# A recurrent layer on one core: the second half's z in three bf16 parts, summed on VectorE

## The chip, the cores and the metric

The kernel runs on one core of a Trainium2 chip. The metric is the device time of one execution in microseconds. Three runs of the kernel before give a median of 1635.45 us.

## The reference

A gated recurrence over 512 steps, for 8 sequences and 512 features, all float32. The input is added to the outputs at the end.

```python
xT = jnp.swapaxes(x, 0, 1)                       # x: (8, 512, 512)
def step(h, x_t):
    fused = jax.nn.sigmoid(jnp.concatenate([x_t, h], axis=-1) @ w_W + w_b)
    hidden_state, output_state = jnp.split(fused, 2, axis=-1)
    memory_state = x_t @ wx_W + wx_b + hidden_state * (h @ wh_W + wh_b)
    h_new = output_state * h + (1.0 - output_state) * jnp.tanh(memory_state)
    return (h_new, h_new)
_, hs = jax.lax.scan(step, h0, xT)
x = x + jnp.swapaxes(hs, 0, 1)
```

Below, r is the gate `hidden_state`, z the gate `output_state`, and m the product `h @ wh_W + wh_b` that r multiplies. Each step needs the h of the step before, so nothing of the recurrence can be done ahead; only the products with x can.

## The kernel before, in words

The 512 features lie as 4 chunks (k = 0 to 3) of 128 partitions. The outputs of a step are made in two halves, o = 0 and o = 1, of two chunks each (W = 64 columns per gate and half). TensorE works with h as the stationary operand, 8 columns (one for each sequence), and the weights as the moving one. Each product is cut into four tiles (j) of 32 array columns side by side, so that each writes 8 rows at 32 j in PSUM, and four matmuls with 64 columns each give 256 features.

Each group has its own PSUM bank: m of the first half (bank 0), r of the first half (1), z of the first half (2), r and m of the second half together (3) and z of the second half (4). ScalarE puts the x products and biases of the step into these banks beforehand (`put_first`, `put_rm`, `put_z`), and all matmuls add to them (`start=False`).

Two kinds of product with h stand side by side:

- `products` (L269 to L276): float32 matmuls of h with `wh`, 8x64, for r, m and z of the first half and for z of the second half. In the order of instructions a step has 64 of them; the trace has two records for each.
- `products_of_parts` (L278 to L287): h in three bf16 parts (24 stationary columns: 8 sequences times 3 parts) with `w_parts`, the weights in three bf16 parts, 24x128, for r and m of the second half. The three parts of h give three groups of 8 rows in PSUM, which VectorE adds (`sum_parts`, L446). GpSimd cuts h into its parts (`part`, L541 to L547), ScalarE and VectorE cut the weights ahead of the loop (L417, L420, L524 to L530).

Of every product the first half of the sum over k (chunks 0 and 1) needs only the first half of h, the second (chunks 2 and 3) only the second half. So TensorE has, in one step (L326 to L353):

```python
r(0, s); m(0, s); z(0, 0, s)     # chunks 0, 1; behind h_ready[0]
products_of_parts(0, s)          # behind parts_ready[0]
r(1, s); m(1, s); z(0, 1, s)     # chunks 2, 3; behind h_ready[1]
products_of_parts(1, s)          # behind parts_ready[1]; rm_done
z(1, 0, s); z(1, 1, s)           # the second half's z; z_done[1]
x_products(s, x_grp[:, s, :])    # a quarter of the next x products
```

The order on each engine is written out by hand, and each engine takes its instructions in that order. When r, m and z of the first half are done, VectorE turns them (32x32 transposes) to features on partitions: `turn_r`, `turn_m`, `turn_z(0)`, L474 to L478. ScalarE takes the sigmoid of r (`reset_first`), VectorE multiplies and adds m (`mix_m(0)`, a scan), ScalarE has the sigmoid of z (`update(0)`) and the tanh (`new(0)`). Then, after rm_done, VectorE has (L482 to L494): `turn_rm`, `sum_parts(0)` (r), `mix_h(0)` (a scan, which gives the first half of h and sets h_ready[0]), `sum_parts(1)` (m), `turn_z(1)`, `mix_m(1)`, `mix_h(1)` (h_ready[1]). ScalarE has in the same time (L396 to L405): `put_first`, `reset_second`, `put_rm`, `update(1)` (sigmoid of z, L375), `new(1)` (tanh, L381), `put_z`. `mix_h` waits for both tanh_ready and z_ready. Once in four steps VectorE adds the bias to the x products behind `mix_h(1)` (`add_bias`, L466). The x products go to a buffer in HBM and back on the DMA queue of SyncE; neither is near the change.

Of the kernel before, what the change touches and what calls it, by code (L numbers as in the profile page):

```python
# [6 lines left out]
ALU = mybir.AluOpType  # L7
# [3 lines left out]
P = 128  # L11
Q = 32


def build(nc, x, h0, w_h, w_x, b_x, b_h, x_rows, out):
# [24 lines left out]
    R_AT = W  # L40
    Z_AT = [2 * W, 3 * W]
    RM_AT = 4 * W
    WHOLE = RM_AT

    M_BANK, R_BANK, RM_BANK = 0, 1, 3
    Z_BANK = [2, 4]
# [18 lines left out]
    with ctx:  # L65
        def sb(name, shape, dt=F32):
            return ctx.enter_context(nc.sbuf_tensor(name, shape, dt))
# [4 lines left out]
        def halves(name):  # L72
            return [sem(f"{name}{o}") for o in range(HALVES)]
# [15 lines left out]
        turned_m = sb("turned_m", [P, ROWS // PAIR, HB, PAIR])  # L89
        turned_rm = sb("turned_rm", [P, 2 * HC, Q])  # L90
        turned_z = sb("turned_z", [P, HALVES, HC, Q])

        summed = sb("summed", [P, 2, HB, PAIR])

# [73 lines left out]
        rm_ahead = sem("rm_ahead")  # L168
        z_ahead = sem("z_ahead")
        r_ready = halves("r_ready")  # L170
        z_ready = halves("z_ready")
        m_pre_ready = halves("m_pre_ready")
        tanh_ready = halves("tanh_ready")
# [86 lines left out]
        @block.tensor  # L260
        def _(pe):
            def x_products(k, stands, bank=X_BANK):

                for j in range(TILES):
                    mm = pe.matmul(ps[Q * j:Q * (j + 1), bank, 0:COLS], stands, wx[:, k, j, :],  # L265
                                   start=(k == 0), stop=(k == KC - 1), tile_position=(0, Q * j))
                return mm

            def products(bank, at, half, s):  # L269


                for k in range(half * HC, (half + 1) * HC):
                    for j in range(TILES):
                        mm = pe.matmul(ps[Q * j:Q * j + B, bank, 0:W], h_of(s - 1, k), wh[:, k, j, at:at + W],  # L274
                                       start=False, stop=(k == KC - 1), skip_group_check=True, tile_position=(0, Q * j))
                return mm  # L276

            def products_of_parts(half, s):  # L278

                for k in range(half * HC, (half + 1) * HC):  # L280
                    for part in range(PARTS):
                        for j in range(TILES):
                            mm = pe.matmul(ps[Q * j:Q * j + PARTS * B, RM_BANK, 0:2 * W], parts_of(s - 1, k),  # L283
                                           w_parts[:, k, part, j], start=False,
                                           stop=(k == KC - 1 and part == PARTS - 1), skip_group_check=True,
                                           tile_position=(0, Q * j))
                return mm  # L287

            def m(half, s):
                return products(M_BANK, M_AT[0], half, s)  # L290

            def r(half, s):
                return products(R_BANK, R_AT, half, s)

            def z(o, half, s):
                return products(Z_BANK[o], Z_AT[o], half, s)

            zeros = h.rearrange("p r o w -> p (r o w)")  # L300
            pe.wait_ge(start_h, 1)
            for n in range(WARM):
                for j in range(TILES):
                    pe.matmul(ps[Q * j:Q * (j + 1), X_BANK, 0:COLS], zeros[:, 0:Q], zeros[:, 0:COLS],
                              start=True, stop=True, tile_position=(0, Q * j))
            for bank in range(X_BANK):
                for j in range(TILES):
                    mm = pe.matmul(ps[Q * j:Q * (j + 1), bank, 0:2 * W], zeros[:, 0:Q], zeros[:, 0:2 * W],
                                   start=True, stop=True, tile_position=(0, Q * j))
            mm.then_inc(bits_set, 1)  # L310
            pe.wait_ge(x0_loaded, 16)
            for k in range(KC):
                pe.wait_ge(wx_loaded[k], 16)
                for g in range(2):
                    last = x_products(k, x_sb[:, k, GT * g:GT * (g + 1)], X_BANK + g)
                    if k == KC - 1:
                        last.then_inc(x_product, 1)
            pe.wait_ge(wh_loaded, KC * 16)
            pe.wait_ge(first_cut, KC)
            pe.wait_ge(second_cut, KC)  # L320
            pe.wait_ge(third_cut, KC)

            with nc.Fori(0, GROUPS, engines=(mybir.EngineType.PE,), hint_back_edge=True) as i:
                t0 = pe.snap(i * RING)
                for s in range(RING):
                    nxt = held(pe, t0 + (s + 1))  # L326
                    pe.wait_ge(h_ready[0], nxt)
                    pe.wait_ge(first_ahead, nxt)
                    r(0, s)
                    if s == 0:  # L330
                        loaded = held(pe, i * 16 + 16)
                    m(0, s)
                    if s == 0:
                        taken = held(pe, i + 2)
                    z(0, 0, s)
                    pe.wait_ge(parts_ready[0], nxt)
                    pe.wait_ge(rm_ahead, nxt)
                    products_of_parts(0, s)
                    pe.wait_ge(h_ready[1], nxt)
                    r(1, s).then_inc(r_done, 1)  # L340
                    m(1, s).then_inc(m_done, 1)
                    z(0, 1, s).then_inc(z_done[0], 1)
                    pe.wait_ge(parts_ready[1], nxt)
                    products_of_parts(1, s).then_inc(rm_done, 1)
                    pe.wait_ge(z_ahead, nxt)
                    z(1, 0, s)
                    z(1, 1, s).then_inc(z_done[1], 1)
                    pe.wait_ge(x_grp_loaded[s], loaded)
                    if s == 0:
                        pe.wait_ge(x_biased, taken)  # L350
                    last = x_products(s, x_grp[:, s, :])
                    last.then_inc(x_used[s] if s < RING - 1 else x_product, 1)

        @block.scalar
        def _(act):
# [7 lines left out]
            def put_z(slot, t):  # L363
                at = Z_AT[1]
                act.activation(ps[:, Z_BANK[1], 0:W], ahead[:, slot, t, at:at + W], ACT.Copy).then_inc(z_ahead, 1)
# [6 lines left out]
                act.activation(m_by[:, 1, :, 1], summed[:, 0, :, 0], ACT.Sigmoid).then_inc(r_ready[1], 1)  # L372

            def update(o):
                act.activation(h_by[:, o, :, 2].rearrange("p (b c) -> p c b", c=HC), turned_z[:, o, :, 0:B], ACT.Sigmoid)\  # L375
                    .then_inc(z_ready[o], 1)

            def new(o, s):
# [5 lines left out]
            def step(i, t0, s):  # L384
                nxt = held(act, t0 + (s + 1))
                slot, t = (s + 1) // RING % SLOTS, (s + 1) % RING
                if t == 0:
                    turn = held(act, (i * (PER_BLOCK // SLOTS) + ((s + 1) // RING // SLOTS + 1)) * LANDED)
                act.wait_ge(r_turned, nxt)
                reset_first()  # L390
                act.wait_ge(z_turned[0], nxt)
                update(0)
                act.wait_ge(m_pre_ready[0], nxt)
                new(0, s)
                if t == 0:
                    act.wait_ge(ahead_loaded[slot], turn)  # L396
                put_first(slot, t)
                act.wait_ge(r_summed, nxt)
                reset_second()
                put_rm(slot, t)  # L400
                act.wait_ge(z_turned[1], nxt)
                update(1)
                act.wait_ge(m_pre_ready[1], nxt)
                new(1, s)
                put_z(slot, t)  # L405

            act.dma_start(bias_x[:, :], b_x).then_inc(bias_x_loaded, 16)
# [24 lines left out]
        def _(dve):  # L432
# [13 lines left out]
            def sum_parts(g):  # L446
                return dve.tensor_reduce(summed[:, g, :, 0].rearrange("p (c b) -> p c b", b=B),  # L447
                                         turned_rm[:, HC * g:HC * (g + 1)].rearrange("p c (w b) -> p c b w", b=B)
                                         [:, :, :, 0:PARTS], AX.X, ALU.add)

            def mix_m(o, add):

                return dve.tensor_tensor_scan(m_pre[:, o].rearrange("p i w -> p (i w)"),  # L453
                                              m_by[:, o].rearrange("p i w -> p (i w)"),
                                              add.rearrange("p i w -> p (i w)"), 0.0, ALU.mult, ALU.add)

            def mix_h(o, s, nxt):

                dve.wait_ge(tanh_ready[o], nxt)
                dve.wait_ge(z_ready[o], nxt)  # L460
                dve.tensor_tensor_scan(h[:, s % RING, o, 0:REGION], h_by[:, o].rearrange("p i w -> p (i w)"),  # L461
                                       h[:, (s - 1) % RING, o, 1:1 + REGION], 0.0, ALU.mult, ALU.add)\
                    .then_inc(h_ready[o], 1)
# [4 lines left out]
            def step(i, t0, s):  # L468
# [22 lines left out]
                dve.wait_ge(x_moved, nxt)  # L491
                dve.wait_ge(m_summed, nxt)
                mix_m(1, summed[:, 1]).then_inc(m_pre_ready[1], 1)
                mix_h(1, s, nxt)  # L494
                if s % RING == RING - 1:

# [143 lines left out]
```

## Time and profile before

| what | value |
|---|---|
| runs | 1635.45 us median of 3 (1634.96 to 1636.28) |
| the profiled execution | 1634.35 us, span 1632.2 us |
| granted TensorE clock, mean | 0.995 |
| TensorE matmul, busy | 1603.5 us, 98% of the span, 94336 records |
| TensorE weight load, busy | 1377.4 us, 84% |
| VectorE, busy | 1162.8 us, 71% |
| ScalarE, busy | 910.0 us, 56% |
| GpSimd, busy | 682.3 us, 42% |
| DMA | 51 GB/s mean |
| chain that ended last | TensorE 97%, DMA 1% |
| of it by line | L274 (float32 products) 56%, L283 (parts) 21%, L265 (x) 20% |

The busy shares are for the whole span, in which some 30 us ahead of the loop are mostly loading. The chain is followed back from the last instruction, at each step to what released it. It says which engine was waited for, not how close the next one was. The time of the profiled execution is 2.1 us above its span; sums are made against 1634.35.

### The profile page before, as it was taken

How to read it: one execution, taken by the hardware profiler on the slowest of the kernel's cores; microseconds unless marked ns; L12 is line 12 of the kernel's file. 1: busy time of each engine (PE TensorE's matmuls, PEld its weight loads, DVE VectorE, ACT ScalarE, POOL GpSimd, SP SyncE). 2: the span in 40 equal slices, each digit the busy share in tenths (PEclk: the TensorE clock that was granted, in tenths of full speed). 3: DMA queues.
4: the chain of work that ended last, by engine and by line, in shares of the span. 5: the costliest groups of instructions: out<-in, count | busy, mean ns of one | idle time of the engine just before them, and what ended most of it. 6: DMA issues, size and time to landing. Idle time of an engine off the chain costs nothing.

```text
span 1632.2 us, 213115 instructions
## 1 busy us (share of the span) xinstructions
PE 1603.5 (98%) x94336; PEld 1377.4 (84%) x94336; DVE 1162.8 (71%) x5782; ACT 910.0 (56%) x4621; POOL 682.3 (42%) x3084
## 2 busy tenths in 40 slices
PE   5899999999999999999999999999999999999998
PEld 3788888888888888888888888888888888888887
DVE  3677777777777777777777777777777777777776
ACT  2455555555555555555555555555555555555555
POOL 1344444444444444444444444444444444444443
PEclk7999999999999999999999999999999999999999
DMA  6111111111111111111111111111111111111111
GB/s 203 31 51 48 52 37 49 47 53 50 47 39 51 49 47 54 37 47 52 51 48 48 40 50 47 52 51 47 39 50 50 47 53 38 48 52 50 49 47 41
DMA packets 194891, 83.29 MB, mean 51 GB/s; under 512 B 123200, under 2 KB 194368, under 8 KB 194880
## 3 DMA queue, kind: packets, MB, share of 16 engines
q1 hardware_dynamic: 193824, 82.47, 18.7%
q10 hardware_dynamic: 1056, 0.67, 0.2%
q8 instruction: 6, 0.10, 0.0%
q14 instruction: 5, 0.04, 0.0%
HBM read 49.30 MB, written 33.75 MB: 51 GB/s over the span
## 4 chain that ended last, share of the span: by engine, by line
PE 97%; DMA 1%; issue 0%; ACT 0%; ACTq 0%; DVE 0%; SPq 0%; POOL 0%; POOLq 0%; DVEq 0%
PE ps L274 56%; PE ps L283 21%; PE ps L265 20%; DMA wx<-in_w_x 1%; DMA x_rows<-xs_biased 0%; ACTq L198 0%; ACT w_parts L417 0%; ACTq L194 0%; ACT w_parts L420 0%; SPq L211 0%; SPq L209 0%; DVE xs_biased L466 0%; DVE h L461 0%; DVE turned_rm L441 0%; POOL y L554 0%
## 5 line engine op out<-in xcount | busy, mean ns | idle before, releaser
L274 PE MATMUL ps<-wh,h 128*8 128x64 f32 x65536 | 1218.0, 219 | 20.0 <-ACT ps L357 14.6
L274 PEld LDWEIGHTS ps<-wh,h 128*8 128x8 f32 x65536 | 1030.9, 92 | 238.8 <-DVE h L461 216.4
L283 PE MATMUL ps<-w_parts,h 128*24 128x128 bf16 x24576 | 544.1, 219 | 0.0
L283 PEld LDWEIGHTS ps<-w_parts,h 128*24 128x24 bf16 x24576 | 442.8, 121 | 0.0
L265 PE MATMUL ps<-wx,x_grp 128*32 128x384 f32 x4096 | 430.7, 486 | 0.0
L368 ACT ACTIVATE m_by<-turned_r 128x16 f32<-128x16 f32 x512 | 112.0, 219 | 561.4 <-DVE turned_r L434 561.4
L544 POOL TENSOR_TENSOR h<-h 128x16 f32<-128x16 f32 x1026 | 224.4, 219 | 365.5 <-DVE h L461 361.9
L461 DVE TENSOR_TENSOR_SCAN h<-h_by,h 128x48 f32<-128x48 f32 x1024 | 260.6, 254 | 160.9 <-ACT h L381 160.9
L576 POOL TENSOR_TENSOR summed<-turned_rm,nothing 128x16 f32<-128x16 f32 x512 | 113.5, 222 | 498.6 <-DVE turned_rm L441 498.6
L434 DVE STREAM_TRANSPOSE turned_r<-ps 128x64 f32<-128x64 f32 x512 | 128.1, 250 | 262.9 <-PE ps L274 258.4
L375 ACT ACTIVATE h_by<-turned_z 128x16 f32<-128x16 f32 x1024 | 238.5, 233 | 117.9 <-DVE turned_z L444 63.2
L546 POOL TENSOR_TENSOR h<-h 128x16 f32<-128x16 f32 x1026 | 225.0, 219 | 80.4
L381 ACT ACTIVATE h<-m_pre 128x32 f32<-128x32 f32 x1024 | 252.7, 247 | 0.0
L444 DVE STREAM_TRANSPOSE turned_z<-ps 128x64 f32<-128x64 f32 x1024 | 247.9, 242 | 2.9 <-PE ps L274 2.9
L447 DVE TENSOR_REDUCE summed<-turned_rm 128x16 f32<-128x48 f32 x1024 | 197.1, 192 | 17.4
L357 ACT ACTIVATE ps<-ahead 128x192 f32<-128x192 f32 x513 | 171.6, 335 | 0.0
L441 DVE STREAM_TRANSPOSE turned_rm<-ps 128x128 f32<-128x128 f32 x512 | 162.1, 317 | 0.3 <-PE ps L283 0.3
L554 POOL TENSOR_TENSOR y<-x_sb,h 128x32 f32 x512 | 137.9, 269 | 0.9
L361 ACT ACTIVATE ps<-ahead 128x128 f32<-128x128 f32 x513 | 135.1, 263 | 0.0
L437 DVE STREAM_TRANSPOSE turned_m<-ps 128x64 f32<-128x64 f32 x512 | 119.5, 233 | 1.5 <-PE ps L274 1.4
L372 ACT ACTIVATE m_by<-summed 128x16 f32<-128x16 f32 x512 | 112.1, 219 | 14.5 <-DVE summed L447 0.4
L453 DVE TENSOR_TENSOR_SCAN m_pre<-m_by,summed 128x32 f32<-128x32 f32 x512 | 115.0, 225 | 0.0
(29 smaller groups left out, 429.4 us busy)
## 6 DMA issues: line engine op xcount, KB each, us to landing
x_rows<-xs_biased SPq DMA_DIRECT2D x128, 192.0 KB, 1.9
ahead<-x_rows SPq DMA_DIRECT2D x512, 32.0 KB
ahead<-x_rows SPq DMA_DIRECT2D x1024, 8.0 KB
x_sb<-in_x SPq DMA_DIRECT2D x34, 256.0 KB, 3.1
x_grp<-in_x SPq DMA_DIRECT2D x516, 16.0 KB, 1.7
out_h<-y SPq DMA_DIRECT2D x32, 256.0 KB, 2.7
wx<-in_w_x SPq DMA_DIRECT2D x4, 768.0 KB, 9.1
wh<-in_w_h SPq DMA_DIRECT2D x4, 512.0 KB, 7.3
```

Source lines behind the costliest of these rows:

```text
L265: mm = pe.matmul(ps[Q * j:Q * (j + 1), bank, 0:COLS], stands, wx[:, k, j, :], start=(k == 0), stop=(k == KC - 1), tile_position=(0, Q * j))
L274: mm = pe.matmul(ps[Q * j:Q * j + B, bank, 0:W], h_of(s - 1, k), wh[:, k, j, at:at + W], start=False, stop=(k == KC - 1), skip_group_check ...
L283: mm = pe.matmul(ps[Q * j:Q * j + PARTS * B, RM_BANK, 0:2 * W], parts_of(s - 1, k), w_parts[:, k, part, j], start=False, stop=(k == KC - 1 ...
L357: act.activation(ps[:, 0:GATES, 0:W], ahead[:, slot, t, 0:GATES * W].rearrange("p (g n) -> p g n", n=W), ACT.Copy).then_inc(first_ahead, 1)
L375: act.activation(h_by[:, o, :, 2].rearrange("p (b c) -> p c b", c=HC), turned_z[:, o, :, 0:B], ACT.Sigmoid)\
L381: act.activation(n_twice, pre.unsqueeze(3).to_broadcast([P, HC, B, 2]), ACT.Tanh)\
L441: return dve.transpose(turned_rm[:, :, :], ps[:, RM_BANK, 0:2 * W].rearrange("p (c q) -> p c q", q=Q))
L444: return dve.transpose(turned_z[:, o], ps[:, Z_BANK[o], 0:W].rearrange("p (c q) -> p c q", q=Q))
L447: return dve.tensor_reduce(summed[:, g, :, 0].rearrange("p (c b) -> p c b", b=B), turned_rm[:, HC * g:HC * (g + 1)].rearrange("p c (w b) - ...
L461: dve.tensor_tensor_scan(h[:, s % RING, o, 0:REGION], h_by[:, o].rearrange("p i w -> p (i w)"), h[:, (s - 1) % RING, o, 1:1 + REGION], 0.0 ...
L544: pool.tensor_tensor(mid(1, s, o), mid(0, s, o), mid_top(0, s, o), ALU.subtract).then_inc(left_once[o], 1)
L546: pool.tensor_tensor(mid(2, s, o), mid(1, s, o), mid_top(1, s, o), ALU.subtract)\
```

## The change

The second half's z goes over from `products` to `products_of_parts`. Its weights are cut into bf16 parts too (`w_rest` and `w_parts` grow from 128 to 192 columns per tile, `wh` shrinks from 256 to 192). z keeps a bank and a group of its own with 64 columns, so a matmul there is 24x64. Its 8-row groups must now be added: `sum_z` on VectorE, between `mix_m(1)` and `mix_h(1)`, into the new tile `pre_z`, with the semaphore z_summed. `update(1)` reads `pre_z`, waits for z_summed, and stands behind `new(1)` on ScalarE. `mix_h(1)` waits for z_ready first and tanh_ready second.

```diff
-    WHOLE = RM_AT
+    WHOLE = Z_AT[1]
...
+        pre_z = sb("pre_z", [P, HC, B])
...
-            def products_of_parts(half, s):
+            def products_of_parts(bank, at, cols, half, s):
 
                 for k in range(half * HC, (half + 1) * HC):
                     for part in range(PARTS):
                         for j in range(TILES):
-                            mm = pe.matmul(ps[Q * j:Q * j + PARTS * B, RM_BANK, 0:2 * W], parts_of(s - 1, k),
-                                           w_parts[:, k, part, j], start=False,
+                            mm = pe.matmul(ps[Q * j:Q * j + PARTS * B, bank, 0:cols], parts_of(s - 1, k),
+                                           w_parts[:, k, part, j, at - WHOLE:at - WHOLE + cols], start=False,
                                            stop=(k == KC - 1 and part == PARTS - 1), skip_group_check=True,
...
-            def z(o, half, s):
-                return products(Z_BANK[o], Z_AT[o], half, s)
+            def z(half, s):
+                return products(Z_BANK[0], Z_AT[0], half, s)
+
+            def second_rm(half, s):
+                return products_of_parts(RM_BANK, RM_AT, 2 * W, half, s)
+
+            def second_z(half, s):
+                return products_of_parts(Z_BANK[1], Z_AT[1], W, half, s)
...
                     pe.wait_ge(parts_ready[1], nxt)
-                    products_of_parts(1, s).then_inc(rm_done, 1)
+                    second_rm(1, s).then_inc(rm_done, 1)
                     pe.wait_ge(z_ahead, nxt)
-                    z(1, 0, s)
-                    z(1, 1, s).then_inc(z_done[1], 1)
+                    second_z(0, s)
+                    second_z(1, s).then_inc(z_done[1], 1)
...
             def update(o):
-                act.activation(h_by[:, o, :, 2].rearrange("p (b c) -> p c b", c=HC), turned_z[:, o, :, 0:B], ACT.Sigmoid)\
+                pre = (turned_z[:, 0, :, 0:B], pre_z[:, :, :])[o]
+                act.activation(h_by[:, o, :, 2].rearrange("p (b c) -> p c b", c=HC), pre, ACT.Sigmoid)\
                     .then_inc(z_ready[o], 1)
...
                 put_rm(slot, t)
-                act.wait_ge(z_turned[1], nxt)
-                update(1)
                 act.wait_ge(m_pre_ready[1], nxt)
                 new(1, s)
+                act.wait_ge(z_summed, nxt)
+                update(1)
                 put_z(slot, t)
...
+            def sum_z():
+                return dve.tensor_reduce(pre_z[:, :, :],
+                                         turned_z[:, 1].rearrange("p c (w b) -> p c b w", b=B)[:, :, :, 0:PARTS],
+                                         AX.X, ALU.add)
+
...
-                dve.wait_ge(tanh_ready[o], nxt)
-                dve.wait_ge(z_ready[o], nxt)
+                for ready in ((tanh_ready[o], z_ready[o]), (z_ready[o], tanh_ready[o]))[o]:
+                    dve.wait_ge(ready, nxt)
...
                 mix_m(1, summed[:, 1]).then_inc(m_pre_ready[1], 1)
+                dve.wait_ge(z_turned[1], nxt)
+                sum_z().then_inc(z_summed, 1)
                 mix_h(1, s, nxt)
```

ScalarE, the second half of a step, before (`summed` is r of the second half, `m_pre` what the tanh is taken of):

```order
L372 ACTIVATE m_by<-summed 128x16 [waits r_summed]
L361 ACTIVATE ps<-ahead 128x128
L375 ACTIVATE h_by<-turned_z 128x2x8 [waits z_turned1]
L381 ACTIVATE h<-m_pre 128x2x8x2 [waits m_pre_ready1]
L365 ACTIVATE ps<-ahead 128x64
```

and with the change:

```order
L380 ACTIVATE m_by<-summed 128x16 [waits r_summed]
L369 ACTIVATE ps<-ahead 128x128
L390 ACTIVATE h<-m_pre 128x2x8x2 [waits m_pre_ready1]
L384 ACTIVATE h_by<-pre_z 128x2x8 [waits z_summed]
L373 ACTIVATE ps<-ahead 128x64
```

The sigmoid of z has moved behind the tanh, and waits for VectorE's sum instead of the transpose.

VectorE, from the second half's sum of m to the end of the step, before (both scans are printed as SCALAR_TENSOR_TENSOR):

```order
L447 TENSOR_REDUCE summed<-turned_rm 128x16
L444 STREAM_TRANSPOSE turned_z<-ps 128x64 [waits z_done1]
L453 SCALAR_TENSOR_TENSOR m_pre<-m_by,summed 128x32 [waits m_summed,x_moved,r_ready1]
L461 SCALAR_TENSOR_TENSOR h<-h_by,h 128x48 [waits z_ready1,tanh_ready1]
L470 REGISTER_ALU
```

and with the change:

```order
L456 TENSOR_REDUCE summed<-turned_rm 128x16
L453 STREAM_TRANSPOSE turned_z<-ps 128x64 [waits z_done1]
L467 SCALAR_TENSOR_TENSOR m_pre<-m_by,summed 128x32 [waits m_summed,x_moved,r_ready1]
L461 TENSOR_REDUCE pre_z<-turned_z 128x16 [waits z_turned1]
L475 SCALAR_TENSOR_TENSOR h<-h_by,h 128x48 [waits tanh_ready1,z_ready1]
L484 REGISTER_ALU
```

One reduction has come in between the two scans; nothing else has changed place.

TensorE, from the second half's r to the x product, before:

```order
L274 MATMUL ps<-wh,h 8x64 [waits h_ready1]
L274 MATMUL ps<-wh,h 8x64 x23
L283 MATMUL ps<-w_parts,h 24x128 [waits parts_ready1]
L283 MATMUL ps<-w_parts,h 24x128 x23
L274 MATMUL ps<-wh,h 8x64 [waits z_ahead]
L274 MATMUL ps<-wh,h 8x64 x15
```

and with the change:

```order
L276 MATMUL ps<-wh,h 8x64 [waits h_ready1]
L276 MATMUL ps<-wh,h 8x64 x23
L285 MATMUL ps<-w_parts,h 24x128 [waits parts_ready1]
L285 MATMUL ps<-w_parts,h 24x128 x23
L285 MATMUL ps<-w_parts,h 24x64 [waits z_ahead]
L285 MATMUL ps<-w_parts,h 24x64 x47
```

The 16 float32 matmuls of the second half's z are 48 bf16 ones in the same place.

## Rows read from the trace of the kernel before

PE is TensorE's matmul, PEld its weight load, DVE VectorE, ACT ScalarE, POOL GpSimd, SP SyncE.

**Rows 1.** Busy us (x records) by engine in a stretch; PE clock, DMA share, GB/s

```profile
100.00:1600.00 1500.00, 1500.00 (x88985) 1294.04 (x88978) 1089.41 (x5443) 854.37 (x4356) 639.69 (x2901) 1.00 0.18 48
```

**Rows 2.** Order in time, PE, one step: start us, us covered, line, xrecords

```profile
801.16 0.64 PE L274 MATMUL ps<-wh,h 128*8 128x64 f32 x32
801.61 0.84 PE L265 MATMUL ps<-wx,x_grp 128*32 128x384 f32 x8
802.25 0.87 PE L274 MATMUL ps<-wh,h 128*8 128x64 f32 x48
802.92 0.53 PE L283 MATMUL ps<-w_parts,h 128*24 128x128 bf16 x24
803.26 0.87 PE L274 MATMUL ps<-wh,h 128*8 128x64 f32 x48
803.93 0.53 PE L283 MATMUL ps<-w_parts,h 128*24 128x128 bf16 x24
804.26 0.25 PE L274 MATMUL ps<-wh,h 128*8 128x64 f32 x4
```

**Rows 3.** Order in time, the first matmuls of the loop

```profile
30.59 1.22 PEld L274 LDWEIGHTS ps<-wh,h 128*8 128x8 f32 x48 [15.29 <-issue]
30.62 1.47 PE L274 MATMUL ps<-wh,h 128*8 128x64 f32 x48 [14.62 <-ACT ps L357]
```

**Rows 4.** Waits: who for whom, us in total, times, longest us

```profile
PEld ps L274 <- DVE h L461: 216.4, 509, 0.4
```

**Rows 5.** Order in time, DVE, ACT and PEld, the step's end

```profile
801.49 0.23 ACT L381 ACTIVATE h<-m_pre 128x32 f32<-128x32 f32 x1
801.61 0.33 ACT L357 ACTIVATE ps<-ahead 128x192 f32<-128x192 f32 x1
...
801.87 0.25 DVE L461 TENSOR_TENSOR_SCAN h<-h_by,h 128x48 f32<-128x48 f32 x1
802.04 0.18 DVE L447 TENSOR_REDUCE summed<-turned_rm 128x16 f32<-128x48 f32 x1
...
802.35 0.23 DVE L453 TENSOR_TENSOR_SCAN m_pre<-m_by,summed 128x32 f32<-128x32 f32 x1
802.41 0.23 ACT L375 ACTIVATE h_by<-turned_z 128x16 f32<-128x16 f32 x1
802.61 0.25 ACT L381 ACTIVATE h<-m_pre 128x32 f32<-128x32 f32 x1
802.75 0.23 ACT L365 ACTIVATE ps<-ahead 128x64 f32<-128x64 f32 x1
802.89 0.26 DVE L461 TENSOR_TENSOR_SCAN h<-h_by,h 128x48 f32<-128x48 f32 x1 [0.32 <-ACT h L381]
803.21 0.73 PEld L274 LDWEIGHTS ps<-wh,h 128*8 128x8 f32 x48
```

**Rows 6.** Order in time, PEld, cut off at 802.20

```profile
802.17 0.11 PEld L274 LDWEIGHTS ps<-wh,h 128*8 128x8 f32 x4 [0.42 <-DVE h L461]
```

**Rows 7.** Order in time, the parts of the second half's h

```profile
803.53 0.22 POOL L546 TENSOR_TENSOR h<-h 128x16 f32<-128x16 f32 x1
...
803.87 0.43 PEld L283 LDWEIGHTS ps<-w_parts,h 128*24 128x24 bf16 x24
```

**Rows 8.** Groups by line: shapes xcount | busy us, mean ns | idle before

```profile
L274 PEld LDWEIGHTS ps<-wh,h 128*8 128x8 f32 x65536 | 1030.9, 92 | 238.8 <-DVE h L461 216.4 <-issue 22.3
L375 ACT ACTIVATE h_by<-turned_z 128x16 f32<-128x16 f32 x1024 | 238.5, 233 | 117.9 <-DVE turned_z L444 63.2
L368 ACT ACTIVATE m_by<-turned_r 128x16 f32<-128x16 f32 x512 | 112.0, 219 | 561.4 <-DVE turned_r L434 561.4
L417 ACT ACTIVATE w_parts<-w_rest 128x512 bf16<-128x512 f32 x4 | 2.2, 617 | 22.0 <-issue 22.0
```

**Rows 9.** Order in time, DVE, the end of a group of four steps

```profile
809.29 0.56 DVE L466 TENSOR_TENSOR xs_biased<-ps,bias_x 128x384 f32<-128x384 f32 x1
810.03 0.25 DVE L434 STREAM_TRANSPOSE turned_r<-ps 128x64 f32<-128x64 f32 x1 [0.18 <-PE ps L274]
```

More of the change, by code:

```diff
@@ L170, in build @@
         r_ready = halves("r_ready")
+        z_summed = sem("z_summed")
         z_ready = halves("z_ready")
@@ L334, in _ @@
                         taken = held(pe, i + 2)
-                    z(0, 0, s)
+                    z(0, s)
                     pe.wait_ge(parts_ready[0], nxt)
                     pe.wait_ge(rm_ahead, nxt)
-                    products_of_parts(0, s)
+                    second_rm(0, s)
                     pe.wait_ge(h_ready[1], nxt)
@@ L341, in _ @@
                     m(1, s).then_inc(m_done, 1)
-                    z(0, 1, s).then_inc(z_done[0], 1)
+                    z(1, s).then_inc(z_done[0], 1)
                     pe.wait_ge(parts_ready[1], nxt)
-                    products_of_parts(1, s).then_inc(rm_done, 1)
+                    second_rm(1, s).then_inc(rm_done, 1)
                     pe.wait_ge(z_ahead, nxt)
-                    z(1, 0, s)
-                    z(1, 1, s).then_inc(z_done[1], 1)
+                    second_z(0, s)
+                    second_z(1, s).then_inc(z_done[1], 1)
                     pe.wait_ge(x_grp_loaded[s], loaded)
```

## The prediction, made before the change was run

> **What bounds the kernel now.** I first read busy time and clock. From 100 to 1600 us TensorE (PE) is busy 1500.00 of 1500.00 us, at a granted clock of 1.00, the 2.4 GHz level [rows 1]; the chain of waits, too, is PE almost throughout (the table above). The reader is to see an engine without a gap in the steady state. But "busy" with modelled ends can hide short waits, so the next view is the order in time [rows 2]. I take start-to-start, never the durations: 48 records are given 0.87 us, but the next kind starts 0.67 after them, since neighbours overlap in the array. A float32 matmul leaves two records. One step runs from the start of the first half's r to the next such start. Its pieces: 48 records of r, m, z from 802.25 to 802.92, 0.67 us; 24 of the parts to 803.26, 0.34; 48 more to 803.93, 0.67; 24 more to 804.26, 0.33; the second half's z, which the change rewrites, 32 records from 801.16 to 801.61, 0.45; the x product, 801.61 to 802.25, 0.64. The sum is **3.10 us**: the period is PE's work alone. 512 x 3.10 = 1587, the first matmul is at 30.62 [rows 3], and the rest of the span is the first steps, at a lower clock.
>
> Is anything just behind PE? PE's weight loads waited for the scan of h 509 times, 216.4 us in all [rows 4]: once in a step, for the first half's h. For the second half's h nothing is recorded. The order in time shows how close both are. The scan of the first half ends at 801.87 + 0.25 = 802.12 [rows 5], the load follows at 802.17 [rows 6] and the matmul at 802.25 [rows 2]. The scan of the second half ends at 802.89 + 0.26 = 803.15, its load follows at 803.21 [rows 5], the matmul at 803.26. A load stands 0.05 to 0.06 before its matmul also where nothing is waited for (parts: load 803.87 [rows 7], matmul 803.93). So the second half's h comes just in time. How little a load needs ahead of its matmul when PE is idle: 30.59 to 30.62, 0.03 us [rows 3]. The slack of the second half is thus 803.26 - 803.21 - 0.03 = **0.02 us**, that of the first half 0.08 - 0.03 = 0.05.
>
> **The change, part by part.**
>
> *PE, second half's z.* 16 float32 matmuls of 64 columns (32 records, 0.45 us) become 48 bf16 ones of 24x64. No row has that shape. Nearest: 24 bf16 pairs of 24x128 take 0.33 to 0.34 us [rows 2], 0.014 each. If the price goes by columns, 48 with half the columns take 0.34; if it goes by pairs, 48 x 0.014 = 0.67. Which? The float32 records of 64 columns take 0.67/48 = 0.014 too. They show only that 0.014 for a pair of load and matmul can be held. The weight loads alone come faster: four in 0.11 us [rows 6], where one takes 0.092 [rows 8], so some 0.006 apart. That is nearer to the low end; I take 0.34 to 0.45, and keep 0.67 for the range. PE's own work becomes 3.10 - 0.45 + 0.34 = 2.99 to 3.10.
>
> The Trainium skill (TensorE: Matmul & The Clock Gate, Back-to-back issue gap) gives columns/2.4 + 2.5 ns for a lone stream, never below about 25 ns, but about 81 ns a matmul at 128 columns for a stream of load and matmul. By that second figure, four tiles side by side, 24 pairs would take 0.49 us; this trace has 0.34, which is the first formula (55.8 ns for four). By the first, the new z would be 12 x 29.2 ns = 0.35 us, an estimate from that page; a pace of loads and matmuls that columns do not lower would be rival (1).
>
> *The wait for the first half's h.* Its scan hangs on rm_done, turn_rm, sum, scan, none of which is changed. PE arriving up to 0.11 sooner can win at most the 0.05 of slack: 3.05.
>
> *ACT and DVE, second half.* This is the term that decides. Before, the sigmoid of z stood ahead of the tanh, 802.41 to 802.64, in time in which ACT waited for the scan of m anyway. That scan ends at 802.35 + 0.23 = 802.58, the tanh starts at 802.61 and ends at 802.86, and the scan of h starts at 802.89 [rows 5]. So the tanh hung on the scan of m, not on the sigmoid, and taking the sigmoid from in front of it wins nothing. Now the sigmoid comes behind the tanh, and the scan of h waits for it. When can it start? (a) For ACT's sake: the next instruction behind the tanh (put_z) starts at 802.75, 0.14 after it. (b) For the sum's sake: DVE gets on 0.17 after the start of the longer scan of h (801.87 to 802.04), so sum_z runs from 802.52 at the latest, takes 0.18 like the second sum of parts, and reaches ACT 0.03 later, at 802.73. So (a) decides, the sum itself is covered with 0.02 to spare, and without this cover its lateness would be added one to one. Sigmoid from 802.75, 0.23 long [rows 8], ends at 802.98; scan of h from 803.01 instead of 802.89: **0.12 us later**. It is bounded from below by a sigmoid of 0.22 (those of r [rows 8]) with a gap of 0.12 (801.49 to 801.61, tanh to put_first): 0.09 later. From above, with a sum that starts when the scan of m has ended (802.58) and so ends at 802.79 with the latency: 0.16 later.
>
> *Who waits for that.* The second half's r, m and z on PE. h ends at 803.27, the load comes at 803.33, the matmul at 803.36 at the earliest: 0.10 after 803.26. From there to rm_done is 72 records as before, and from rm_done to the scans the same path as before: the ring closes, and PE's 0.11 saved lies outside it, between rm_done and h. The period is 3.10 + 0.12 - 0.02 = **3.20 us**. Bounds: 3.10 + 0.09 - 0.02 = 3.17 and, with all the lateness and no slack, 3.10 + 0.16 = 3.26. PE, on its own at 2.99 to 3.10, is below it and waits 0.1 to 0.2 in each step.
>
> *Neighbours.* The parts on POOL hang on the same h: the second subtraction, from 803.53, is done at 803.75, where the load of parts is at 803.87 [rows 7]; POOL moves by 0.12, the load by 0.10, covered. add_bias on DVE, once in four steps, ends at 809.29 + 0.56 = 809.85, ahead of the turn of r at 810.03 [rows 9]; both move alike, covered. put_z is later by 0.12 and used over a microsecond later: nothing. turn_z sits behind sum_parts(1) on DVE, long after z's end: nothing.
>
> *Ahead of the loop.* w_rest grows from 512 to 768 columns. The eight casts on ACT lead to put_first and to the first matmul. ACT's slope, from a cast of 512 columns [rows 8] and put_z's 64 [rows 5], is (617 - 230)/448 = 0.86 ns a column, so 256 more cost 0.22 us each, 8 x 0.22 = **1.8 us**. DVE's subtractions between them grow at a like rate and keep ahead. Bounds 0 and 4.
>
> *Sum.* 512 steps x 0.10 = 51.2, and 1.8: 1634.35 + 53.0 = 1687.4 for an execution like the profiled one (span 1632.2, 2.1 around it); the median shown, 1635.45, is 1.1 above it, so **1688.5**. Case bounds: 512 x 0.07 + 0 gives 1671; 512 x 0.16 + 4 gives 1721, of which I keep up to 1716, the last 0.01 needing every bound at once.
>
> **The rivals.**
>
> (1) *A pair has a price of its own.* If 48 pairs of 64 columns take 0.67, PE needs 3.32 a step: 512 x 0.22 + 2 = 115, 1750 us. It decides from the point where z takes more than 0.45 + 0.10 = 0.55. For it: all pairs of the trace cost 0.014. Against it: the loads 0.006 apart, and x records that cost 0.08, so columns count. 10%.
>
> (2) *Faster: ACT overlaps tanh and sigmoid so that h is not late.* In this kernel h would have to be on time within the 0.02 of slack, so the sigmoid would have to end by 802.88 and start by 802.65. Then PE's saving counts up to the first half's wait: 3.05, 1634 - 512 x 0.05 + 2 = 1611. It is decided by the gap between two activations, which would have to be 0.04 and is 0.12 to 0.14 in the rows. 6%.
>
> (3) *A wash.* PE's loads in fact have more slack than 0.02 and z costs about what it did, or the two ends meet: 1634 to 1639. 4%. For it speaks only that starts in the rows have two decimals.
>
> **How the numbers follow.** Forecast 80%, rivals 10, 6 and 4. A measurement of this kernel can tell about 0.2%, 3.3 us, from no change. The range goes over the likeliest case, with its bounds 1671 and 1716, and leaves the rivals' 20% out. Slower is 80 + 10 = 90; faster 6; same 4.
>
> **What would show it.** In the profile after: PE's loads wait for h about 1000 times, not 509, since now the second half's are among them; the sigmoid of the second half's z starts 0.14 behind the tanh, and the scan of h 0.15 after the tanh's end instead of 0.03; PE has idle time in each step; the period is 3.20; 48 records of z in 0.34 to 0.45; put_first 1.8 later. The prediction is wrong if the scan of h still starts on the tanh's end, if z's 48 records take over 0.55, or if r's loads follow h without moving their matmuls.

## The result, and the profile after

The changed kernel takes 1692.03 us (median of 4, 1690.71 to 1692.47) against 1635.2 us (median of 4, the three runs above and one more): a ratio of 1.0341, 95% interval 1.0329 to 1.0354. The time forecast was 1688.5, with a range of 1671 to 1716. The profiled execution has a span of 1690.2 us, 58.0 more than before. The table puts the few numbers side by side.

| what | before | after |
|---|---|---|
| span, us | 1632.2 | 1690.2 |
| steady period of a step, us | 3.102 | 3.208 |
| first matmul of the loop, us | 30.62 | 33.24 |
| PE's loads waited for the scan of h | 509 times, 216.4 us | 509 times, 176.5 us |
| PE busy from 100 to 1600 us | 1500.00 | 1500.00 |

The period is taken from ScalarE's sigmoid of r, which comes once in a step. These are its 101st and 501st occurrence in the order in time, first of before, then of after (start us, us, line):

```profile
351.27 0.22 ACT L368 ACTIVATE m_by<-turned_r 128x16 f32<-128x16 f32 x1 [1.14 <-DVE turned_r L434]
1591.93 0.22 ACT L368 ACTIVATE m_by<-turned_r 128x16 f32<-128x16 f32 x1 [1.14 <-DVE turned_r L434]
```

```profile
365.23 0.22 ACT L376 ACTIVATE m_by<-turned_r 128x16 f32<-128x16 f32 x1 [1.14 <-DVE turned_r L443]
1648.60 0.22 ACT L376 ACTIVATE m_by<-turned_r 128x16 f32<-128x16 f32 x1 [1.14 <-DVE turned_r L443]
```

1240.66/400 = 3.102 and 1283.37/400 = 3.208. All periods below are taken in this way. (Between one step and the next this row alternates, 3.01 and 3.19 before, so only a mean over many steps is of use.) 512 steps of 0.107 more are 55 us, and the loop starts 2.6 us later: together 57 of the 58.0.

Where in the step are the 0.107? The order in time of PE, after, over more than one step; it answers to [rows 2]:

```profile
1000.35 1.08 PE L285 MATMUL ps<-w_parts,h 128*24 128x128 bf16 x72
1001.22 0.85 PE L267 MATMUL ps<-wx,x_grp 128*32 128x384 f32 x8
1001.87 0.87 PE L276 MATMUL ps<-wh,h 128*8 128x64 f32 x48
1002.54 0.54 PE L285 MATMUL ps<-w_parts,h 128*24 128x128 bf16 x24
1002.88 0.87 PE L276 MATMUL ps<-wh,h 128*8 128x64 f32 x48
1003.55 1.07 PE L285 MATMUL ps<-w_parts,h 128*24 128x128 bf16 x72
```

Parts and z now share a line, so 72 records stand together: 24 of the parts and 48 of z. They take 1001.22 - 1000.35 = 0.87 us, of which the parts are 0.33 or 0.34: **z takes 0.53 to 0.54**, where 32 float32 records took 0.45. (The mean over the 467 steps between 100 and 1600 us is 0.546.) The x product takes 0.65. All the other pieces are 0.67, 0.34, 0.67, and above all there is no gap of any kind ahead of the second half's r: 1002.88 is 0.34 behind 1002.54, as before. The step's sum is 0.67 + 0.34 + 0.67 + 0.34 + 0.54 + 0.65 = 3.21, again PE's work alone.

So the second half's h does not hold up the matmuls. The waits, after, say the same; they answer to [rows 4]:

```profile
PEld ps L276 <- DVE h L475: 176.5, 509, 0.5
DVE h L475 <- ACT h_by L384: 163.6, 512, 0.3
ACT h L390 <- DVE m_pre L467: 123.2, 512, 1.3
```

509 waits, once in a step, where the forecast had about 1000. The second row shows that the scan of h now does hang on the sigmoid of z, as forecast, and the third that the tanh hangs on the scan of m. Then why is nothing late? The step's end in the order in time, after, to be read beside [rows 5]:

```profile
1001.39 0.25 DVE L475 TENSOR_TENSOR_SCAN h<-h_by,h 128x48 f32<-128x48 f32 x1
...
1001.88 0.22 DVE L467 TENSOR_TENSOR_SCAN m_pre<-m_by,summed 128x32 f32<-128x32 f32 x1
...
1002.02 0.18 DVE L461 TENSOR_REDUCE pre_z<-turned_z 128x16 f32<-128x48 f32 x1
...
1002.14 0.25 ACT L390 ACTIVATE h<-m_pre 128x32 f32<-128x32 f32 x1 [0.24 <-DVE m_pre L467]
1002.27 0.22 ACT L384 ACTIVATE h_by<-pre_z 128x16 f32<-128x16 f32 x1
...
1002.52 0.26 DVE L475 TENSOR_TENSOR_SCAN h<-h_by,h 128x48 f32<-128x48 f32 x1 [0.32 <-ACT h_by L384]
...
1002.83 0.21 PEld L276 LDWEIGHTS ps<-wh,h 128*8 128x8 f32 x11
```

From the first half's scan to the second's it is 1002.52 - 1001.39 = 1.13 us, before 802.89 - 801.87 = 1.02: the second half's h is 0.11 later, close to the 0.12 forecast. But PE started its step later by as much: the first half's r is 1001.87 - 1001.39 = 0.48 behind the first half's scan, before it was 0.38. Both ends have moved by a tenth, and meet in the same way as before: the load at 1002.83, 0.05 behind the end of the scan, the matmul at 1002.88. The reader sees two delays side by side, of which only the larger one counts. What the smaller one would be worth by itself, no view of this profile tells.

### The profile page after: what moved, and what is told of

The parts are those of the page before. It is cut to its first block, busy times and chain, and to the rows that moved or that the text cites. A ratio compares the mean times of both kernels' runs of the same rounds, so it can differ in the third digit from the quotient of the medians.

```text
span 1690.2 us, 230011 instructions
## 1 busy us (share of the span) xinstructions
PE 1657.6 (98%) x102528; PEld 1441.8 (85%) x102528; DVE 1215.7 (72%) x6294; ACT 862.6 (51%) x4621; POOL 683.6 (40%) x3084
## 4 chain that ended last, share of the span: by engine, by line
PE 97%; DMA 1%; issue 0%; ACT 0%; ACTq 0%; DVE 0%; SPq 0%; POOL 0%; POOLq 0%; DVEq 0%
PE ps L276 41%; PE ps L285 37%; PE ps L267 20%; DMA wx<-in_w_x 1%; DMA x_rows<-xs_biased 0%; ACT w_parts L426 0%; ACTq L200 0%; ACT w_parts L429 0%; ACTq L196 0%; SPq L213 0%; SPq L211 0%; DVE xs_biased L480 0%; DVE h L475 0%; DVE m_pre L467 0%; DVE turned_rm L450 0%
## 5 line engine op out<-in xcount | busy, mean ns | idle before, releaser
L276 PEld LDWEIGHTS ps<-wh,h 128*8 128x8 f32 x49152 | 772.9, 92 | 227.9 <-DVE h L475 176.5
L276 PE MATMUL ps<-wh,h 128*8 128x64 f32 x49152 | 885.5, 219 | 16.5 <-ACT ps L365 16.5
L285 PE MATMUL ps<-w_parts,h 128*24 128x128 bf16 (+1 forms) x49152 | 820.2, 214 | 3.9 <-issue 3.9
L285 PEld LDWEIGHTS ps<-w_parts,h 128*24 128x24 bf16 x49152 | 739.3, 130 | 3.0 <-issue 3.0
L384 ACT ACTIVATE h_by<-turned_z 128x16 f32<-128x16 f32 x512 | 120.2, 235 | 93.7 <-DVE turned_z L453 58.7
```

Of the source, the lines that this page charges most:

```text
L285: mm = pe.matmul(ps[Q * j:Q * j + PARTS * B, bank, 0:cols], parts_of(s - 1, k), w_parts[:, k, part, j, at - WHOLE:at - WHOLE + cols], star ...
```

## The experiments

Ten kernels. Two theories at the start. RING is the prediction's: the late h of the second half sets the period. PRICE: TensorE's new z costs 0.54 instead of 0.45, and nothing else matters. The change has both, so each was run alone. `mix_h(1)` waits in each kernel for z_ready and tanh_ready in the order that stands with the sum or the new order on ScalarE (z_ready first), and in the order of before where both are taken out; the excerpts of the diffs below show neither this nor the declarations.

**ring_only**: the kernel before, with VectorE's sum and the new order on ScalarE.

```diff
+    dve.wait_ge(z_turned[1], nxt)
+    sum_z().then_inc(z_summed, 1)     # behind mix_m(1)
...
-    act.wait_ge(z_turned[1], nxt)
-    update(1)
     act.wait_ge(m_pre_ready[1], nxt)
     new(1, s)
+    act.wait_ge(z_summed, nxt)
+    update(1)                         # reads pre_z
```

> The float32 z of before, with the sum on VectorE and ScalarE's new order, nothing changed on TensorE. Theory RING (the prediction's: the late h of the second half sets the period): h is 0.12 us late, slack 0.02, period 3.20, some 1686 us; TensorE's loads wait for h twice in a step. Theory PRICE (the change lost its time only in TensorE's new z, 0.55 us instead of 0.45, and the second half's h has enough slack for 0.12): period 3.10 to 3.12, 1635 to 1645 us.

Measured: 1662.53 us, ratio 1.0168 (1.0151 to 1.0185), period 3.157. Neither number: half of what RING said, and clear of PRICE. The order in time of PE shows the wait, and its size:

```profile
800.38 0.85 PE L276 MATMUL ps<-wh,h 128*8 128x64 f32 x48
801.05 0.52 PE L285 MATMUL ps<-w_parts,h 128*24 128x128 bf16 x24
801.43 0.86 PE L276 MATMUL ps<-wh,h 128*8 128x64 f32 x48
802.11 0.52 PE L285 MATMUL ps<-w_parts,h 128*24 128x128 bf16 x24
802.44 0.63 PE L276 MATMUL ps<-wh,h 128*8 128x64 f32 x32
```

From the parts to the second half's r it is 0.38 instead of 0.34, and the 48 records behind take 0.68 instead of 0.67. Here are the scan that they wait for, the sigmoid it hangs on, and the load, from the same run:

```profile
800.73 0.25 ACT L384 ACTIVATE h<-m_pre 128x32 f32<-128x32 f32 x1 [0.23 <-DVE m_pre L461]
800.87 0.21 ACT L378 ACTIVATE h_by<-pre_z 128x16 f32<-128x16 f32 x1
...
801.11 0.26 DVE L469 TENSOR_TENSOR_SCAN h<-h_by,h 128x48 f32<-128x48 f32 x1 [0.32 <-ACT h_by L378]
801.43 0.68 PEld L276 LDWEIGHTS ps<-wh,h 128*8 128x8 f32 x48
```

The sigmoid starts 0.14 behind the tanh, as forecast. The scan ends at 801.37, the load starts at 801.43 and the matmul at 801.43 too. When PE's next matmul waits for h, it needs no 0.03 us behind its load but next to none. The slack in the kernel before was 803.26 - 803.21 = 0.05, not 0.02. And the scan of h is 0.10 later, not 0.12. The medians over the steps of the loop close the sum: from the first half's scan to the second's 1.022 us before and 1.126 here, from the end of the scan to the matmul 0.104 before and 0.055 here. 0.104 later, less 0.049 of slack, is the 0.055 that the period grew by. Note too that the waits are 510 (217.7 us) in this run, once in a step, although the second half's h holds PE up in each step too: the loads of the parts are recorded until 801.42, and the next load starts at 801.43, so no idle time lies between them. A lateness of this size does not show in the count that the prediction named as its sign; a larger one does, as sum_old_order below shows.

**price_only**: the changed kernel without the sum, with ScalarE's order of before. z of the second half is taken from the first of its three parts of h alone.

```diff
-    dve.wait_ge(z_turned[1], nxt)
-    sum_z().then_inc(z_summed, 1)
...
+    act.wait_ge(z_turned[1], nxt)
+    update(1)                         # reads turned_z[:, 1, :, 0:B]
     act.wait_ge(m_pre_ready[1], nxt)
     new(1, s)
-    act.wait_ge(z_summed, nxt)
-    update(1)
```

> The bf16 z of the change on TensorE, but without the sum on VectorE and with ScalarE's order of before (z of the second half is taken from the first of its three parts alone). Theory PRICE: 48 records of z take 0.55 us as with the change, period 3.20 to 3.22, 1688 to 1692 us. Theory RING alone: with h on time again the kernel is at 1634 to 1640 or, if z were cheap, at 1611.

Measured: 1692.75 us, ratio 1.0353 (1.0336 to 1.037), period 3.210. That is the whole of the change's time with nothing of its ring (scan to scan is 1.022 again, on the median). PRICE holds for the change; the ring is real but hidden under it.

If so, then with a cheaper z the ring must come out as the next bound, at the 3.157 of ring_only. **two_parts** is the change with two of the weights' three parts for z (it leaves out the smallest part), and **two_parts_price** is the same without sum and reordering.

```diff
-    for part in range(PARTS):
+    for part in range(parts):         # 2 for second_z, 3 for second_rm
...
-    stop=(k == KC - 1 and part == PARTS - 1), ...
+    stop=(k == KC - 1 and part == parts - 1), ...
```

> The change as it is, but the second half's z uses two of the three parts of the weights: 32 pairs instead of 48, some 0.37 us (it leaves out the smallest part of these weights). Theory TWO BOUNDS (the new z's price sets 3.21, and right behind it the late h sets 3.16, as in the run with the ring alone): TensorE falls to 3.04, the ring is what is left, period 3.16, 1663 to 1667 us. Theory PRICE ALONE (the late h is harmless once z is cheap): below 1635 us.

> The same 32 pairs without the sum and with ScalarE's order of before. Theory TWO BOUNDS: nothing is late, and TensorE gets as far as the wait for h allows, period 3.03 to 3.06: 1600 to 1616 us. If a load of z's kind also costs outside its own stretch, more.

Measured: two_parts 1665.96 us, ratio 1.0185 (1.0168 to 1.0202), period 3.159. two_parts_price 1615.1 us, ratio 0.9871 (0.9854 to 0.9887), period 3.059. The first is the ring as measured by itself (1662.53), with a first matmul at 31.86 us instead of ring_only's 30.31, and 0.002 us more a step. The second shows what a z of this price (32 records take 0.36 us) brings when the second half's h is on time. There TensorE waits for the first half's h: its scan ends at 1001.04, the load and the matmul follow:

```profile
1000.79 0.25 DVE L475 TENSOR_TENSOR_SCAN h<-h_by,h 128x48 f32<-128x48 f32 x1
1001.09 0.28 PEld L276 LDWEIGHTS ps<-wh,h 128*8 128x8 f32 x16 [0.46 <-DVE h L475]
```

That is the bound which the prediction had put at 3.05. Both kernels leave a part of the weights out, and the second also the sum, so neither computes the layer.

**Is it the sum or the order on ScalarE** that makes h late? **act_order_only** is the kernel before with `new(1)` ahead of `update(1)`, and no sum. **sum_old_order** is the kernel before with the sum, and `update(1)`, waiting for z_summed, ahead of `new(1)`.

```diff
-    act.wait_ge(z_turned[1], nxt)
-    update(1)
     act.wait_ge(m_pre_ready[1], nxt)
     new(1, s)
+    act.wait_ge(z_turned[1], nxt)
+    update(1)
```

> The kernel before with nothing but ScalarE's order of the change (tanh ahead of the sigmoid of z) and no sum. If the gap between two activations decides when the sigmoid starts and the sum is covered (the prediction's (a)), it costs what the ring alone cost: 0.055 a step, 1660 to 1665 us. If the sum decides, the sigmoid starts sooner and this is at 1635 to 1650 us.

```diff
-    act.wait_ge(z_turned[1], nxt)
+    act.wait_ge(z_summed, nxt)
     update(1)                         # reads pre_z
     act.wait_ge(m_pre_ready[1], nxt)
     new(1, s)
```

> The kernel before with the sum of z on VectorE, but ScalarE's order of before (sigmoid of z, then tanh). The sigmoid cannot start before the sum, and the tanh is queued behind it: the scan of h is some 0.25 us later than before, less the slack of 0.05 some 0.20 a step, 1725 to 1745 us. If the order on ScalarE does not matter, as with the new order: 1662 us.

Measured: act_order_only 1663.06 us, ratio 1.0167 (1.015 to 1.0184), period 3.157: the same as with the sum. The sum costs nothing where it stands; the order costs all of it. sum_old_order 1750.11 us, ratio 1.0701 (1.0683 to 1.0719), period 3.329. This is a little above the range given. The wait for the second half's h is now 0.17 longer than in ring_only, and here the count does show it: PE's loads wait for the scan of h 1016 times, 313.3 us. The step's end of sum_old_order in the order in time:

```profile
801.23 0.18 DVE L455 TENSOR_REDUCE pre_z<-turned_z 128x16 f32<-128x48 f32 x1
801.23 0.22 POOL L556 TENSOR_TENSOR h<-h 128x16 f32<-128x16 f32 x1
801.45 0.23 ACT L378 ACTIVATE h_by<-pre_z 128x16 f32<-128x16 f32 x1 [0.34 <-DVE pre_z L455]
801.57 0.24 ACT L384 ACTIVATE h<-m_pre 128x32 f32<-128x32 f32 x1
...
801.91 0.26 DVE L469 TENSOR_TENSOR_SCAN h<-h_by,h 128x48 f32<-128x48 f32 x1 [0.49 <-ACT h L384]
```

ScalarE sits idle for 0.34 us until the sum is there, with the tanh behind it whose input was ready. The tanh ends at 801.81 and the scan comes 0.10 after it, where 0.03 is usual (0.101 and 0.032, medians of this run and of before). The trace has the reason. Of two waits ahead of the scan, VectorE's sequencer takes one as an instruction of its own and the other with the scan. This kernel kept the change's order of the two waits, so the wait for the tanh, here the last to come, is the one taken by itself: at 801.842, 0.04 behind the tanh, and the scan starts 0.065 behind that. In the kernel before and in ring_only the one taken by itself is the one that comes early. Given that the sum has to be made, the new order on ScalarE is the better of the two: it saves 0.17 us a step against the old. But some 0.07 of this (0.101 - 0.032) belong to the order of the two waits, an estimate from these rows; the old order on ScalarE with the waits as before was not run.

**What sets the price of the new z?** Four kernels, all built on price_only, so that the second half's h is not late. In **price_8rows** the loads of z take 8 stationary columns (the first part of h), in **price_16rows** 16. In **price_32cols** each matmul has 32 moving columns (half of z's outputs get no product with h). In **price_contig** 24 stationary columns are read from neighbouring elements of the weights; h's product is left out of that z.

```diff
-    pe.matmul(ps[Q * j:Q * j + PARTS * B, bank, 0:cols], parts_of(s - 1, k), ...
+    pe.matmul(ps[Q * j:Q * j + rows, bank, 0:cols], parts_of(s - 1, k)[:, 0:rows], ...   # rows = 8 or 16
...
-    return products_of_parts(Z_BANK[1], Z_AT[1], W, half, s)
+    return products_of_parts(Z_BANK[1], Z_AT[1], W // 2, half, s)                        # price_32cols
...
-    pe.matmul(ps[Q * j:Q * j + PARTS * B, bank, 0:cols], parts_of(s - 1, k), ...
+    pe.matmul(ps[Q * j:Q * j + PARTS * B, Z_BANK[1], 0:W], w_parts[:, k, 0, j, 0:PARTS * B], ...   # price_contig
```

> As price_only, but the second half's z loads 8 stationary columns instead of 24 (only the first part of h is multiplied). If the width of the weight load sets the price of a 24x64 pair, z falls to 0.35 us, TensorE then waits for the first half's h, period 3.05 to 3.07, some 1612 to 1622 us. If each pair has a price of its own, z stays at 0.55 us and the time at 1690.

> As price_only, but each matmul of the second half's z has 32 moving columns instead of 64 (half of z's outputs are left without their product with h). If load or pair sets the price, z stays at 0.55 us and the time near 1690. If columns have a share in it, z falls, by up to 12 x 13.3 ns = 0.16 us, to 0.39 us and the time to some 1612 to 1622 us.

> As price_only, with 16 stationary columns loaded for the second half's z (two parts of h). Four matmuls side by side took 0.046 us with 24 columns and 0.029 with 8, where 64 columns alone give 0.029. If the time grows evenly with the columns loaded, 16 are at 0.031 to 0.038 and the step at 3.13 to 3.17; if 24 crosses a threshold, 16 behave like 8.

> As price_only, but the 24 stationary columns of the second half's z are read from neighbouring bf16 elements (of the weights; h's product is left out of that z) instead of h's, which lie 24 bytes apart. If the reading at a stride makes the loads slow, z falls to 0.35 to 0.45 us and the time to 1612 to 1640. If the number of columns alone does, z stays at 0.54 and the time at 1690.

Measured, one run each: price_8rows 1650.46 us (period 3.130), price_16rows 1653.67 (3.131), price_contig 1651.84 (3.130), price_32cols 1689.81 (3.203). So half the moving columns change next to nothing, and the load is what counts; but not by its number of columns alone, since 24 neighbouring ones are as good as 8 spread ones. (price_contig also reads another tile than the others, the weights and not h; a spread read of the weights, which would tell the spacing from the tile, was not run.) The groups by line of the weight loads (mean ns of one) show it for each kernel. The changed kernel first, whose row holds both kinds of 24-column loads, those of z and those of r and m:

```profile
L285 PEld LDWEIGHTS ps<-w_parts,h 128*24 128x24 bf16 x49152 | 739.3, 130 | 3.0 <-issue 3.0
```

price_8rows, r and m's loads and then z's:

```profile
L285 PEld LDWEIGHTS ps<-w_parts,h 128*24 128x24 bf16 x24576 | 450.7, 121 | 1.5 <-issue 1.5
L285 PEld LDWEIGHTS ps<-w_parts,h 128*8 128x8 bf16 x24576 | 273.3, 92 | 2.0 <-issue 2.0
```

price_16rows, z's loads:

```profile
L285 PEld LDWEIGHTS ps<-w_parts,h 128*16 128x16 bf16 x24576 | 280.7, 110 | 2.2 <-issue 2.2
```

price_contig, z's loads (L307 is that kernel's line for them):

```profile
L307 PEld LDWEIGHTS ps<-w_parts 128*24 128x24 bf16 x24576 | 271.1, 92 | 2.0 <-issue 2.0
```

A load of h's parts with 24 columns is 121 ns, with 16 it is 110, with 8 it is 92, and 24 columns that lie side by side are 92 as well. In the changed kernel z's loads must be at 2 x 130 - 121 = 139 on the mean, and the trace has 139 for them: they queue. The four matmuls side by side follow each other every 0.056 us with 128 moving columns, and there is time for four such loads; z's four take 0.546/12 = 0.046 us, and with 32 moving columns (price_32cols) 0.045.

One thing stays open. With light loads z should take some 0.35 us, if 64 columns cost half of 128, and takes more. This is PE's order in time in price_contig, where z has a line of its own, first in one step and then two steps later:

```profile
1001.87 0.55 PE L285 MATMUL ps<-w_parts,h 128*24 128x128 bf16 x24
1002.20 0.60 PE L307 MATMUL ps<-w_parts 128*24 128x64 bf16 x48
1002.61 0.88 PE L267 MATMUL ps<-wx,x_grp 128*32 128x384 f32 x8
1003.28 0.83 PE L276 MATMUL ps<-wh,h 128*8 128x64 f32 x45
...
1008.42 0.58 PE L307 MATMUL ps<-w_parts 128*24 128x64 bf16 x48
1008.98 0.85 PE L267 MATMUL ps<-wx,x_grp 128*32 128x384 f32 x8
```

In the first of these steps z takes 0.41, and the x product 0.67 instead of 0.64. With these pieces a step would take 3.09, not the 3.130 measured. Most of the rest comes from one step in four, the second shown here: z takes 0.56. It is the step in which PE also waits for VectorE's add_bias (`x_biased`) ahead of the x product. That was done more than 1 us before, yet no load runs for 0.08 us between the last of z's and the first of the x product's. On the mean over the loop z takes 0.44 and the x product 0.68. All three kernels with light loads end at the same period, 3.130 or 3.131, which is above the 3.059 of two_parts_price with its 32 heavy pairs. Something else than the loads holds 48 short pairs in a row, and something holds the one step in four; what they are was not tried. My 1612 to 1622 us for price_8rows and 1612 to 1640 for price_contig missed for that reason.

None of these kernels is faster than the kernel before and does the whole computation. With z's parts summed between the two scans and the sigmoid behind the tanh, as here, h comes late by 0.055 a step net of the slack, whatever TensorE saves on z, and that alone is 1.7% (ring_only, two_parts). Other places for the sum, ahead of the scan of m or on GpSimd, were not tried.

## Why the prediction was right in its number and wrong in its bound

- *PE sets the period before, without a gap*: right, 3.102.
- *Slack of the second half's h, 0.02*: too small. ring_only has 0.05, since a waiting matmul starts with its load. The 0.03 was taken from one row at the loop's start, where the granted clock was 0.50, the lower level (1.2 GHz).
- *h 0.12 later because the sigmoid stands behind the tanh, the sum covered*: the mechanism is right in each link (act_order_only is as slow as ring_only; the sigmoid 0.14 behind the tanh). The size was 0.10, because the sigmoid takes 0.217 us behind the tanh and not 0.233. It is the place that counts, not what is read: act_order_only's sigmoid of `turned_z` takes 0.217 there too, and sum_old_order's of `pre_z`, ahead of the tanh, 0.232. Together with the slack the term is 0.055 a step, not 0.10: some 28 us, not 51.
- *The new z costs 0.34 to 0.45*: this step failed. It is 0.54, because the loads of 24 spread columns come every 0.046 us for four, not every 0.029. The prediction took the low end for being nearest to a row on loads: four of 8 columns, 0.006 apart. The row that was nearest in kind was another, the loads of 24 strided columns behind the parts, and it could show no more than that they fit into 0.056. Half of that width was taken for granted.
- *Which bound wins*: so the order of the two was turned round. The cases were ring 3.20 above PE's 2.99 to 3.10; measured, they are PE 3.21 above ring 3.16. The change's time is rival (1), a price of the pair, at a middle price (0.011 instead of 0.014 us, set by the load): 0.54 lies just below the 0.55 from which the prediction said it would decide, and decides, because the ring was lower than thought. That the sum 1688.5 is within 4 us of 1692.03 is a coincidence of 0.107 from one cause and 0.10 forecast for another.
- *Ahead of the loop, 1.8 us*: 2.6. The casts themselves grew as forecast: four took 3.04 us instead of 2.19 and four 3.02 instead of 2.17, 1.7 in all. The rest is that they started at 26.70 instead of 25.80, behind ScalarE's DMA issues. That part is no property of the change: price_8rows and two_parts, the same up to the loop, have their first matmul of it at 31.82 and 31.86, and price_only at 33.32.
- *Neighbours*: right; GpSimd's parts, add_bias and put_z showed up nowhere.
- *Signs*: of those named, "509 becomes about 1000" and "idle time on PE" were not seen, and the scan of h 0.15 behind the tanh's end was (1002.52 against 1002.39, 0.13). The first sign looked as if it told at once that the ring did not bind; but in ring_only it stayed at 510 with the ring binding. It shows a wait of the size of sum_old_order's (1016 times) and not one of 0.05. The sign to trust is the start-to-start time in which the wait would lie.

The formula of the Trainium skill (TensorE: Matmul & The Clock Gate, Back-to-back issue gap), columns/2.4 + 2.5 ns, gave 0.35 for z. It fits the pairs of 128 columns, and not these: the trace has 0.54. The same page (LDWEIGHTS) lets the time of a load depend on its columns alone. The trace agrees on loads of h's parts that more columns take longer, 92, 110 and 121 ns for 8, 16 and 24, but has 92 for 24 neighbouring ones of the weights, so columns alone do not give the time.

## What to carry to other kernels

When a wait's lateness is put on a path, measure the other side too: a delay in the engine that is waited on and a delay in the engine that waits overlap, and only the larger moves the time; run each alone before you name one. Where a new instruction shape has no row, ask for each of its resources (moving columns, load, issue) what its nearest row merely fits into, since a cost that is hidden under 128 columns may be the bound under 64. And look for a wait in the start-to-start time of the pieces, not in the count of waits.

## What the runs showed of the hardware that was not expected

- TensorE weight loads with the same number of columns differ in time: 24 bf16 columns of h 24 bytes apart are recorded at 121 ns, 24 of the weights side by side at 92 ns, as long as 8 columns 24 bytes apart. The kernel with the side-by-side loads is some 40 us faster than the one with the spread ones (1651.84, one run, against 1692.75). Spacing and tile changed together.
- Where TensorE's next matmul waits for h, load and matmul start within the same 0.01 us (801.43 in ring_only, 0.055 behind the end of the scan), where 0.05 lies between them in a full stream.
- Of two semaphores waited for ahead of one VectorE instruction, it matters which comes last: 0.032 us from the last producer's end to the scan in the kernel before, 0.101 in sum_old_order, where the late one was taken as a wait of its own.
- ScalarE starts the next small activation 0.12 to 0.14 us after the last one started, though each is recorded at 0.22 to 0.25, so the order of two activations costs 0.10 and not 0.22.
